# A hybrid convolution, attention and FFN kernel: attention order written out, late weightings, token 0 and weight products moved up, and filler products on TensorE

## The reference

```
x = x + conv51x51_depthwise(groupnorm(x))
t = tokens(x)                                  # (16, 256, 32)
t = t + masked_attention(ln(t))                # mask: local, every 16th, first 4, and "spiking" keys
h = ln(t)
for step p in 33 steps:                        # weights differ by step and by op
    op = argmax(h[0, 0, :19])                  # token 0 of sample 0 chooses
    if am[p, op]: h = softmax(q k^T / sqrt(32)) v wo    with q = h wq, k = h wk, v = h wv
    if fm[p, op]: h = relu(h w1 + b1) w2 + b2
t = t + h
```

## Time and profile before

| what | us |
|---|---|
| median of 3 runs | 188.16 (186.61 to 189.0) |
| profiled execution, its own time | 189.25 |
| span of the profiled execution | 187.2 |
| PE busy | 154.1 (82%) |
| DVE busy | 110.9 (59%) |
| ACT busy | 90.0 (48%) |
| POOL busy | 63.1 (34%) |
| mean granted TensorE clock | 0.910 of 2.4 GHz |

### The profile page before, as it was taken

How to read it: one execution, slowest core, us unless ns; L and a number is a source line. 1 busy time by engine, 2 the same in 40 slices (tenths; PEclk the granted TensorE clock), 3 DMA queues, 4 the chain that set the end, 5 groups by cost and what they waited for, 6 DMA issues and landing times.

```text
span 187.2 us, 4295 instructions
## 1 busy us (share of the span) xinstructions
PE 154.1 (82%) x1422; PEld 94.5 (50%) x1423; DVE 110.9 (59%) x258; ACT 90.0 (48%) x180; POOL 63.1 (34%) x157
## 2 busy tenths in 40 slices
PE   7999988699519899996999876988956986898842
PEld 5878653335305656564543554655514555565410
DVE  1461589619968689477417275587663165496673
ACT  3554412327502433474316358685651448775751
POOL 2770000100905796502200075747000076755000
PEclk9999999969985999999555999999997599999996
DMA  5999100000000000000000000000010000000003
GB/s 143 339 173 160 28 4 1 2 0 0 7 0 0 2 3 0 0 9 21 0 0 14 18 0 3 0 3 2 0 30 2 0 0 0 0 0 0 0 0 112
DMA packets 4170, 5.03 MB, mean 27 GB/s; under 512 B 633, under 2 KB 3513, under 8 KB 4154
## 3 DMA queue, kind: packets, MB, share of 16 engines
q1 hardware_dynamic: 4010, 4.57, 11.1%
q10 hardware_dynamic: 144, 0.25, 0.4%
HBM read 2.73 MB, written 0.53 MB: 17 GB/s over the span
## 4 chain that ended last, share of the span: by engine, by line
PE 52%; DVE 24%; ACT 8%; issue 7%; POOL 3%; DVEq 2%; DMA 1%; SPq 1%; ACTq 0%; POOLq 0%
PE bank L576 7%; PE bank L558 6%; DVE sinv L1332 6%; PE bank L590 5%; PE bank L644 5%; PE bank L596 4%; ACT shifted L958 4%; DVE mem L1285 4%; PE bank L842 4%; PE bank L663 3%; PE bank L541 3%; PE bank L629 2%; PE bank L624 2%; PE bank L786 2%; POOL shifted L461 2%
## 5 line engine op out<-in xcount | busy, mean ns | idle before, releaser
L461 POOL TENSOR_SCALAR shifted<-shifted,nmax 128x256 f32<-128x256 f32 x96 | 44.7, 484 | 42.7 <-DVE nmax L1327 33.1
L971 ACT ACTIVATE big<-bank 128x512 f32<-128x512 f32 x48 | 27.6, 602 | 21.3 <-PE bank L576 21.3
L1327 DVE TENSOR_REDUCE nmax<-shifted 128x2 f32<-128x512 f32 x32 | 21.5, 684 | 22.8 <-ACT shifted L958 22.5
L576 PE MATMUL bank<-ident,shifted 128*128 128x128 f32 x192 | 26.9, 280 | 3.4 <-ACT big L971 2.7
L576 PEld LDWEIGHTS bank<-ident,shifted 128*128 128x128 f32 x192 | 20.5, 141 | 12.4 <-issue 8.3
L958 ACT ACTIVATE shifted<-bank 128x512 f32<-128x512 f32 x32 | 19.3, 604 | 9.7 <-PE bank L558 9.7
L1332 DVE RECIPROCAL sinv<-bank 128x256 f32<-128x256 f32 x12 | 21.0, 1751 | 3.1 <-PE bank L596 3.1
L1323 DVE CUSTOM_DVE_ANT_0 shifted<-bank,negm 128x256 f32<-128x256 f32 x32 | 11.3, 420 | 3.1 <-PE bank L558 3.0
L1108 ACT ACTIVATE big<-bank,wfs 128x512 f32<-128x512 f32 x16 | 9.9, 686 | 6.6 <-PE bank L842 6.6
L590 PE MATMUL bank<-big,v 128*32 128x256 f32 x192 | 12.9, 385 | 0.0
L596 PE MATMUL bank<-big,onesc 128*32 128x256 f32 x192 | 12.7, 381 | 0.0
(11 more groups left out here) (170 smaller groups left out, 223.6 us busy)
## 6 DMA issues: line engine op xcount, KB each, us to landing
big<-filt SPq DMA_DIRECT2D x8, 192.0 KB, 6.8
xrev<-xrev_dram SPq DMA_DIRECT2D x1, 512.0 KB, 5.0
xin<-xtok_dram SPq DMA_DIRECT2D x1, 512.0 KB, 5.2
out_dram<-outT SPq DMA_DIRECT2D x2, 256.0 KB, 2.2
maskc<-maskc_dram SPq DMA_DIRECT2D x1, 256.0 KB, 5.3
kx<-kx_dram ACTq DMA_DIRECT2D x1, 248.0 KB, 3.0
wf<-wf_dram SPq DMA_DIRECT2D x3, 81.0 KB, 2.8
wx<-wx_dram SPq DMA_DIRECT2D x1, 216.0 KB, 3.8
```

Source lines behind the costliest of these rows:

```text
L461: last = nc.gpsimd.tensor_scalar(sh[b % NSH][:, ih, :], sh[b % NSH][:, ih, :], -1.0 if masked else 1.0, nmax[:, b, ih:ih + 1], ALU.mult, A ...
L576: mm = pe.transpose(bank[4 + b % 2][:, jh * S + ih * P:jh * S + (ih + 1) * P], sh[b % NSH][:, ih, jh * P:(jh + 1) * P], ident)
L971: nc.scalar.activation(flat(probT[b]), bank[4 + b % 2][:, :], ACT.Exp).then_inc(s_P, 1)
L1327: m = nc.vector.tensor_reduce(nmax[:, b, :], sh[b % NSH][:, :, :], AX.X, ALU.max, negate=True)
```

## The change

- The order of the round's PE work is written out sample by sample (below). The row sums (`sums_pe`) and the products with the values (`weigh_pe`) are two functions now, with a turn between them. The products of group 2 come after the last turn.
- In the steps, ACT's copy of the scores and DVE's reduction are gone: DVE uses the instruction of the masked attention, with a mask of zeros (`nomask`), straight from PSUM.
- In the steps, queries and values are interleaved (`STEPPRE`), drained by ACT alone, and the values of groups 2 and 3 come during the turns.
- The value bias of the masked attention is a product of a row of ones with `bvo` that opens the accumulation of the values on PE; POOL's eight additions (L487) are gone.
- The transposes for the residual (K_RES) come before the spikes, and ACT drains them before its exponentials.
- Fillers: 4 before the spike current; 4 for each of the sweeps 5 to 9, each set behind a wait for its sweep; 2 for each of the five check links; 2 more; and 12 instead of 6 after the spike count. In a kind-3 step: 4 after the last weighting, 2 before and 2 after the weight products.
- Token 0's hidden unit moves to between turns 13 and 14 in a step, its row to right after the last turn, and in the FFN step to after two of four strips. The second pair of outputs, the next weight products and their diagonals: outputs 0 and 1 now come after the second hidden products, the weight products before outputs 2 and 3, the diagonals before the last drain.
- After the masked attention DVE makes output 2 before it picks the op; POOL adds both residuals after its last sample.

```diff
+        LIF_LINK = 13
+        LIF_CHECK = 5
+        FILLED_FROM = 5
...
-        def attention_pe(pe, base, t, k0, keys, ahead, masked):
...
+        def attention_pe(pe, at, t, k0, keys, between):
...
+            def scores(g):
+                wait(pe, s_nm, at.samples, GB * g)
+                scores_pe(pe, range(GB * g, GB * (g + 1)), keys)
...
+            turn(0)
+            scores(1)
+            turn(1)
+            turn(2)
+            between(2)
+            turn(3)
+            turn(4)
+            between(4)
+            scores(2)
+            turn(5)
+            turn(6)
+            sums(0)
+            turn(7)
+            weigh_pe(pe, 0)
+            turn(8)
+            scores(3)
+            turn(9)
+            turn(10)
+            sums(1)
+            turn(11)
+            weigh_pe(pe, 1)
+            turn(12)
+            turn(13)
+            between(13)
+            turn(14)
+            turn(15)
...
             def values(t, k, src, g, w):
                 t.fill_wait(pe, k)
+                biased = t is st
+                if biased:
+                    pe.matmul(t.bank(k)[:, 0:S], onesr[:, :], rep(bvo[0:1, :], NH * GB), start=True, stop=False)
...
+            spare(SPAREB, 4)
             st.drained(pe, K_CUR)
...
             def before_spikes():
 
                 scores_pe(pe, (0, 1, 2, 3), kt)
+                for h in range(NH):
+                    transposed_pe(pe, K_RES + h, tok, h)
+                for i in range(FILLED_FROM, LIF_ITERS):
+                    pe.wait_ge(s_dve, LIF_LINK + 2 * i)
+                    spare(bank[5], 4)
+                for n in range(1, LIF_CHECK + 1):
+                    pe.wait_ge(s_dve, LIF_LINK + 2 * LIF_ITERS + n)
+                    spare(bank[5], 2)
+                spare(bank[5], 2)
                 pe.wait_ge(s_spk, 1)
                 st.fill_wait(pe, K_CNT)
                 pe.matmul(st.bank(K_CNT)[:, 0:S], onesb[:, :], spk[:, :], start=True, stop=True).then_inc(s_task, 1)
-                for h in range(NH):
-                    transposed_pe(pe, K_RES + h, tok, h)
-                spare(bank[5], 6)
+                spare(bank[5], 12)
...
                 with pe.If(kind == 3):
...
+                    token0_row(STEP0)
+                    sums_pe(pe, at, t, len(LPRE), 2)
+                    weigh_pe(pe, 2)
                     t.drained(pe, K_HF - 1)
-                    token0(r)
-                    hidden(r, 0)
-                    token0_row()
-                    weigh_pe(pe, att, t, len(LPRE), NG - 1)
+                    hidden(r, 0, range(GB), (0, GB - 1))
+                    sums_pe(pe, at, t, len(LPRE), NG - 1)
+                    weigh_pe(pe, NG - 1)
+                    spare(bank[4], 4)
+                    next_step(pe, b, reg_r, reg_op, reg_code)
                     k = K_HF + GB + 1
-                    t.drained(pe, k - 1)
-                    outputs(t, k, (0, 1))
                     t.drained(pe, k)
-                    hidden(r, 1)
-                    next_step(pe, b, reg_r, reg_op, reg_code)
-                    t.drained(pe, k + 2 + GB)
-                    outputs(t, k + 2 + GB, (2, 3))
-                    weight_products()
+                    hidden(r, 1, range(GB), None)
+                    outputs(t, k + GB, (0, 1))
+                    spare(bank[2], 2)
+                    t.drained(pe, k + 2)
+                    weight_products(STEPP)
+                    spare(bank[2], 2)
+                    t.drained(pe, k + GB)
+                    outputs(t, k + GB + 2, (2, 3))
```

More of the change, by code:

```diff
@@ L339, in drained, with upto @@
                 wait(eng, s_dd, self.d, count("D", self.owners[:k]))
-        st = Tasks(STATIC, y0=K_ATT)
+        st = Tasks(STATIC, banks=[8 - RING + k % RING for k in range(K_ATT)])
+        def upto(b, members):
+            return sum(m <= b for m in members)
         def rep(ap, n):
@@ L448, in _, with __init__, round_registers, rounds @@
             sp.wait_ge(s_out, 32)
-        def attention_pool(pool, masked, between, reg_att=None):
+        class Rounds:
+            def __init__(self, samples=0, attentions=0):
+                self.samples, self.attentions = samples, attentions
+        FIRST = Rounds()
+        def round_registers(eng, name):
+            regs = [eng.alloc_register(f"{name}_{n}") for n in ("samples", "attentions")]
+            for reg, n in zip(regs, (B, 1)):
+                eng.reg_mov(reg, n)
+            return regs
+        def rounds(eng, regs):
+            return Rounds(*(eng.snap(reg) for reg in regs))
+        def next_round(eng, regs):
+            for reg, n in zip(regs, (B, 1)):
+                eng.reg_alu(reg, reg, n, ALU.add)
+        def attention_pool(pool, between, reg_att=None):
             for b in range(B):
-                if masked:
+                if reg_att is None:
                     pool.wait_ge(s_nm, b + 1)
@@ L578, in turn_pe, with sums_bank, sums_pe @@
             mm.then_inc(s_T, 1)
-        def weigh_pe(pe, base, t, k0, g):
+        def sums_bank(t, g):
+            return bank[5] if g == NG - 1 and t is not st else bank[YBANKS[g % 2]]
+        def sums_pe(pe, at, t, k0, g):
+            out = sums_bank(t, g)
             t.drained(pe, k0 + max(g - 1, 0))
-            if t is st and g == 0:
-                pe.wait_ge(s_vb, NG * NH)
-            wait(pe, s_P, base, GB * (g + 1))
-            out = bank[YBANKS[g % 2]]
-            for jh in range(NH):
-                for q in range(GB):
-                    b = g * GB + q
-                    pe.matmul(out[q * C:(q + 1) * C, 0:S], v[:, jh, b, :], probT[b][:, jh, :],
-                              start=(jh == 0), stop=(jh == NH - 1), tile_position=(0, q * C))
+            made(pe, at, g * GB + GB - 1)
             if t is st:
@@ L1051, in _ @@
             nc.scalar.activation(table[:, :], eps[0:1, :], ACT.Exp)
-            attention_act(act, 0, True)
+            for h in range(NH):
+                st.filled(act, K_RES + h)
+                nc.scalar.activation(outT[:, :, h * P:(h + 1) * P], st.bank(K_RES + h)[:, :].rearrange("p (g s) -> p g s", g=NG),
+                                     ACT.Identity, bias=bor).then_inc(s_da, 1)
+            attention_act(act, FIRST, lambda b: None)
             def squared(g):
@@ L1101, in token0 @@
                     act.wait_ge(s_h0, ffns)
[L1102 removed]
+                    nc.scalar.activation(h0[:, :], into[:, 0:1], ACT.Relu, bias=b1s).then_inc(s_h0r, 1)
                     act.reg_alu(reg_ffns, reg_ffns, 1, ALU.add)
```

352 lines of the change are left out of this document (194 added, 158 removed).

## The result

The changed kernel took 183.38 us (median of 4, 181.42 to 184.92) against 187.66 us (median of 4): ratio 0.9623, 95% interval 0.950 to 0.975. In a second series, run as `c_after` beside three experiments, it was 181.45 against 186.61 us, ratio 0.9588 (0.953 to 0.965). Every ratio in this document is of the fast executions alone (those within 1.5% of the fastest of their kernel), whereas the medians are of all of them. So it is about 4% faster by the ratios, 2.3% and 2.8% by the medians. Forecast were 6.5%, 176.0 us; the ratio times the 188.16 us of before gives 181.1, at the upper edge of the range (181.5), and the median itself lies above it.

The account below looks back on a forecast made before the run. The prediction saw the step round held by a hand-over through four engines, not one engine. Its terms, +2.0 - 2.4 + 0.15 - 5.7 + 0.5 - 5.7 - 2.3 + 1.3 = -12.15 us, gave 176.0 us from 188.16; range 170.0 to 181.5.

Parts of the forecast that it names:

- Step rounds: Both attention step rounds, first query to last turn: 22.0 us against 27.7, so -5.7 us each.
- Step end: From a step's last turn to the next queries: net +0.5 us; at the last step's end +1.3 us.
- E: The end of a step's last turn, the zero point from which the forecast times the step's end.
- Clock at the second step: Second step's first stretch, before at half clock: full clock after the change, -2.3 us, at worst 0.
- The current: The spike current's product before the spikes: 1.7 us at full clock instead of 3.42, so -1.7 us.
- The count: PE's count of spikes, queued behind 32 fillers: at 57.6 instead of 55.60, +2.0 us with the current's gain included.
- scores 1.15, eight transposes 1.1: PE's work after the values and before the 32 fillers ahead of the count, in us.
- The second rival: Fillers hold the clock neither at the current nor at the step's end: 181 us, chance 0.12.
- the slower rival: Fillers before the count run at half clock, the clock down since 37.2: count near 75, total 196 us, chance 0.04.
- Masked round: From the count to the masked attention's last turn: 22.3 us instead of 24.7, so -2.4 us.
- Group norm and FFN step: After the masked round: +0.4 us for the later op, -0.25 for the FFN op picked sooner; +0.15 in the sum.
- The rival of a clock that stays up: The clock stays full after the masked round, first step starting 4.7 us sooner: 171.3 us, chance 0.25.

Follow-up runs that it names:

- the order alone: The changed kernel with all fillers that the change added left out, the order and everything else kept: 178.05 us, ratio 0.9421.
- the best version without fillers: The changed kernel with a 128-row value bias, whole strips, the op before output 2 and no filler beyond the kernel before's: 173.72 us, ratio 0.9246.
- C: The changed kernel itself, unaltered, to which the follow-up edits were made: 183.38 us, ratio 0.9623; in a second series 181.45 us, ratio 0.9588.
- the version with 128 rows: The changed kernel with only the value bias product altered, to 128 rows of 1/128 instead of one row of ones: 179.98 us, ratio 0.9667.
- the one-row version whose clock held: The 170.53 us combination of edits (whole strips, early op, fewer fillers before the count, group norm fillers), with the one-row value bias again: 171.34 us, ratio 0.9172.

## Why the prediction was half right

**The number.** Of the 12.15 us forecast 7.1 came by the ratio. That it still lies inside the range, by 0.4 us, is luck: the range reached up to 181.5 for a clock that falls at the current and at the step's end, and there it held. What took the time were three other places, named below.

**Step rounds: right in size, half of the reason.** 22.2 us against 22.0 forecast. The reason given was the hand-over through ACT's copy. With the copy gone and the old loop a round took 24.85 us, so half of the saving, 2.7 us, came from the written-out order, which I had not priced by itself (1.7 net of what it moves to the step's end). The other 2.8 came with the copy's removal and the interleaved queries and values, which no run separates.

**Step end: right in kind.** Last hidden products at E + 6.6 (forecast 6.8), last outputs at E + 10.4 (10.7), next query at E + 12.7 (12.1); the branch on PE took 1.2 us of issue instead of 0.3. Of the 1.1 us that the end became longer the fillers around the weight products are 0.7: without them it is 11.9 us, against 11.5 before. In the last step the outputs came at E + 9.7 (10.0). Another 1.0 us of the tail lies behind DVE's last instruction, in the store of the result (3.55 us from there to the end, 2.5 before); nothing in the change touches it, it took 3.1 us in `c_after` and up to 4.5 us in the other profiles, and it is not explained.

**Clock at the second step: right, but not through the fillers.** It was also full in both profiles without fillers at the steps' ends, the order alone and the best version without fillers.

**The current: right in size** (1.89 us), and again at full clock in the same two profiles, which have no fillers there either. So the reason given, fillers that hold the clock, is not borne out at either place.

**The count: right in its mechanism, wrong in its size.** The step that failed is "scores 1.15, eight transposes 1.1", together with the values at 1.1 each, all priced at full clock. The clock was at a half from 47.5 to 54.3 us, although PE was never idle. From the end of the current to the first of the fillers before the count the forecast had 11.8 us; C took 15.2 (38.86 to 54.01), the version with 128 rows 11.0 (37.91 to 48.95), and the one-row version whose clock held 12.2 (37.66 to 49.83). So about 3 us of the miss are the clock and 0.4 the slower pace of the one-row pairs. The second rival, a clock that falls where fillers were to hold it, named the current and the step's end, not this place; the slower rival came nearest, but its clock was down from 37 us on. The 32 fillers took 7.24 us, as forecast (6.9 to 7.7), and the count came at 61.19 instead of 57.6: 3.6 us, the largest part of the 8 us that are missing between the two profiles. Right was that POOL's additions held up the spikes by 0.9 us.

**Masked round: half.** 23.4 us from the count to token 0 against 22.3. Scores wait for the fourth maximum twice (0.37 us each), and exponentials or POOL hold two turns (0.34 each); I had counted no such gaps. The 1.2 us that the round gained are not the order's, for at full clock the old loop needs 23.5 us. Before, it ran at half clock up to 61.2 us, and that is worth about as much: the best version without fillers, at half clock up to 59.6 us, took 24.3 us for it instead of 23.4.

**Group norm and FFN step: wrong.** The sum had "the op of the FFN step is picked about 1 us sooner", from strips that each take a quarter. They run beside each other; the row came no sooner and splitting cost PE 1.2 us. The late op cost 0.7 us instead of 0.4. Together +1.7 instead of +0.15; whole strips and the early op gave back 0.6 and 0.7 us of it, each in a run of its own, and the rest is not assigned.

**The rival of a clock that stays up** was priced at 4.7 us; the fillers in the group norm gave 4.5.

The Trainium skill ("TensorE: Matmul & The Clock Gate", the part on the gate) ties the clock to how busy PE has been and advises against idle gaps. The traces agree in kind for the group norm, where C's PE waited 1.18, 0.47, 0.56 and 0.41 us and fillers in such waits kept the clock up in three of four profiles, though the gaps that the page warns of are longer. They differ for the values, where PE was busy 4.00 of 4.00 us and the clock fell.

## What to carry to other kernels

Fillers are instructions in an in-order queue: put them only where the engine would wait anyway, count how many fit, and remember that a wait in front of a group doesn't pace it if the engine arrives late. Look both for a hand-over through an engine that can be left out and for a better order on the busiest engine: in a round of this kernel they gave 2.8 and 2.7 us. Before moving a small product ahead of others, look whether those run beside each other, for then it isn't ahead of anything. And look at the granted clock of every execution before you compare two kernels: here one fall more or less was worth as much as most of the edits (4.5 us in the group norm).

## What the runs showed of the hardware

- PE's clock fell to a half while PE was busy all the time, with products of one stationary row between the value products (8 of 9 profiles); with as many products of 128 rows it did not (3 of 3).
- The two instructions of the one-row bias product and the four of the value product behind them took 1.25 us together at full clock, with 128 rows 0.88 us.
- Two 32-row strips of 512 columns take as long as four: 2.26 us at half clock in both cases.
- Hidden products of 32 rows, 102.4 to 106.1 us in C and 95.5 to 100.5 us in the kernel before, ran at half clock throughout; it came back during the outputs behind them (at 109.0 and 102.2 us).
- The scan of 16 x 256 on DVE took 0.82 us beside POOL's additions and 0.68 us without them; the spikes were ready 0.9 us later for it.
